# Attention stage: scores of the next sequence and probabilities of this one in one TensorE step

## The reference, cut to what matters

```python
x = x + layernorm(attn(layernorm(x), Wq, bq, Wk, bk, Wv, bv, Wo, bo))

def attn(x, ...):                       # B=16 sequences, S=256, hidden=256
    q = (x @ Wq.T + bq).reshape(B, S, 16, 16)   # 16 heads of 16
    k = (x @ Wk.T + bk).reshape(B, S, 4, 16)    # 4 key and value heads
    v = (x @ Wv.T + bv).reshape(B, S, 4, 16)
    q, k = rope(q), rope(k)
    scores = q @ k.T * 0.25, causal mask        # 4 query heads share a key head
    return (softmax(scores) @ v) @ Wo.T + bo
```

## Time and profile before

| | us |
|---|---|
| median of 3 runs | 2287.17 |
| lowest, highest run | 2286.58, 2296.49 |
| profiled execution | 2282.91 |
| its span, first to last instruction | 2281.2 |
| of that, from the first mask of the scores to the end of the attention stage (23.7 to 551.7) | 528.0 |

### The profile page before, as it was taken

The page is one execution under the profiler, slowest core; times in us unless marked ns, Lnnn a source line. Parts: engine busy times, 40 slices in busy tenths (PEclk is TensorE's granted clock), DMA queues, the critical chain, the costliest instruction groups (busy, mean ns, idle before and its releaser), DMA issues.

```text
span 2281.2 us, 35483 instructions
## 1 busy us (share of the span) xinstructions
PE 2082.8 (91%) x10450; PEld 1487.2 (65%) x10499; DVE 1319.4 (58%) x3916; ACT 740.1 (32%) x1495; POOL 271.7 (12%) x427
## 2 busy tenths in 40 slices
PE   7999999997599888884599999999999999999998
PEld 3544455444577555553377887778877788778887
DVE  3565665654533222222867777677777777677653
ACT  1233323332144322232333333333433343333321
POOL 1000000001055233332000000000000000000000
PEclk9899989988599999997689999999999999999999
DMA  9800000000022222224011101111011110111100
GB/s 341 160 1 0 0 0 0 0 0 1 2 93 92 74 76 78 76 76 175 14 52 56 52 17 45 56 56 51 5 56 56 51 56 5 56 56 38 42 21 31
DMA packets 75715, 120.74 MB, mean 53 GB/s; under 512 B 18672, under 2 KB 59760, under 8 KB 75120
## 3 DMA queue, kind: packets, MB, share of 16 engines
q1 hardware_dynamic: 68720, 100.91, 13.8%
q0 software_dynamic: 6912, 18.92, 2.3%
HBM read 81.71 MB, written 38.08 MB: 53 GB/s over the span
## 4 chain that ended last, share of the span: by engine, by line
PE 83%; issue 5%; DVE 5%; DMA 4%; ACT 2%; POOL 1%; SPq 0%; DVEq 0%; POOLq 0%; ACTq 0%
PE bank L184 21%; PE bank L193 11%; PE bank L1146 5%; PE bank L1175 5%; DMA moe_rows<-sorted_in 4%; PE bank L561 3%; PE bank L1185 3%; PE bank L1620 2%; PE bank L617 2%; PE bank L1646 2%; PE bank L1108 2%; PE bank L579 2%; PE bank L637 2%; PE bank L524 2%; PE bank L1599 2%
## 5 line engine op out<-in xcount | busy, mean ns | idle before, releaser
L184 PE MATMUL bank<-moe_xT,up_w 128*128 128x256 f32 x2304 | 554.1, 384 | 0.0
L184 PEld LDWEIGHTS bank<-moe_xT,up_w 128*128 128x128 f32 x2304 | 435.0, 191 | 70.3 <-issue 11.6
L193 PE MATMUL bank<-down_w,moe_hT 128*128 128x256 f32 x1152 | 307.6, 390 | 18.4 <-ACT moe_y L230 18.4
L227 ACT ACTIVATE moe_silu<-bank 128x256 f32<-128x256 f32 x288 | 110.6, 384 | 641.2 <-PE bank L184 641.2
L193 PEld LDWEIGHTS bank<-down_w,moe_hT 128*128 128x128 f32 x1152 | 202.9, 190 | 55.2 <-issue 26.5
L1325 DVE TENSOR_REDUCE q_slots<-bank 128x4 f32<-128x1024 f32 (+1 forms) x96 | 116.3, 1222 | 126.2 <-PE bank L1146 126.2
L1251 ACT ACTIVATE probs<-bank 128x1024 f32<-128x1024 f32 x96 | 98.4, 1025 | 201.1 <-PE bank L1175 201.1
L617 PE MATMUL bank<-up_w,moe_xT 128*128 x320 | 115.7, 485 | 25.3 <-issue 24.8
L1146 PE MATMUL bank<-kT,qT 16*128 16x256 f32 (+1 forms) x1024 | 125.4, 377 | 0.0
L293 DVE TENSOR_TENSOR moe_silu<-moe_silu,up_w 128x256 f32<-128x256 f32 x192 | 81.3, 423 | 75.2 <-ACT moe_silu L227 71.8
L1861 DVE TENSOR_TENSOR_SCAN m<-bank,delta 128x256 f32<-128x256 f32 x128 | 86.6, 677 | 64.7 <-PE bank L1660 63.4
(11 more groups left out here) (291 smaller groups left out, 3262.9 us busy)
## 6 DMA issues: line engine op xcount, KB each, us to landing
up_w<-comb_rows SPq DMA_DIRECT2D x32, 768.0 KB, 5.2
comb_got<-results SPq DMA_DIRECT2D x16, 768.0 KB, 7.9
moe_rows<-sorted_in SPq DMA_DIRECT2D x80, 128.5 KB
sorted_in<-zero SPq DMA_DIRECT2D x10, 1024.0 KB, 9.2
down_w<-comb_rows SPq DMA_DIRECT2D x16, 512.0 KB, 7.8
up_w<-in_up SPq DMA_DIRECT2D x2, 3168.0 KB, 14.1
up_w<-in_up SPq DMA_DIRECT2D x2, 2304.0 KB, 13.0
results<-moe_y SPq DMA_DIRECT2D x32, 128.0 KB
```

Of the source, the lines that this page charges most:

```text
L184: last = mm(k.bank[:, UP_BANK + i % 3, half * S:(half + 1) * S], m.w_up[:, c, at + half * m.inter:at + (half + 1) * m.inter], m.xT[:, par, ...
L193: last = mm(k.bank[:, SUM_BANK, j * D:(j + 1) * D], m.hT[:, i % 3, j * P:(j + 1) * P], m.w_down[:, m.expert(i), :], start=(i == 0 and j == ...
L227: nc.scalar.activation(m.silu[:, i % 3, :], k.bank[:, UP_BANK + i % 3, 0:S], ACT.Silu).then_inc(m.silu_ready, 1)
```

## The change

- A new step `pair` takes the place of `scores` and `probs` on TensorE. It issues, for i = 0 to 5, the scores of unit i of sequence t + 1 and the probabilities of unit i XOR 1 of sequence t, alternating. Since i and i XOR 1 are on different heads, the four products address the four row groups.
- PSUM is dealt out anew: banks 0 and 1 for scores, 2 and 3 for probabilities, 4 and 5 for `av`, 6 (`MIX_BANK`) for `turn_x`, `qkv`, `turn_att` and now `proj`, 7 for all turns of q and k. Scores have one pair of banks instead of two, and so have probabilities: pair i waits for the maxima and the exponentials of pair i - 1.
- `av` is three steps of four heads instead of six of two; `probs` has four buffers.
- `xn` and `z` (the two normalisations) move from VectorE to ScalarE, as an activation with a scale and a shift; GpSimd makes the shift with two small operations more. The residual (`add`) moves from VectorE to GpSimd. The copy of v (`copy_v`) moves from VectorE to ScalarE. The four additions of q in `rope` become one, the eight multiplications of `att` two.
- A sequence is now in work over five periods (norm at t - 3, statistics at t + 2); the table is walked from t = -1 to 17.

The core of the diff:

```diff
 ORDER = (
-    (0, "scores", 0), (0, "scores", 1), (0, "scores", 2), (0, "turn_m", 0), (-1, "att", 0), (-1, "turn_av", 1),
...
+    (0, "pair", 0), (1, "scores", 0), (0, "probs", 0), (-1, "turn_av", 1), (-1, "att", 0), (2, "qkv", 0), (1, "copy_v", 0),
+    (-2, "z", 0),
+    (0, "pair", 1), (1, "scores", 1), (0, "probs", 1), (2, "rope", 0), (-1, "turn_att", 0), (-2, "add", 0), (0, "av", 0),
+    (0, "pair", 2), (1, "scores", 2), (0, "probs", 2), (3, "norm", 0), (0, "copy_av", 0), (2, "qkv", 1), (1, "turn_m", 0),
+    (0, "pair", 3), (1, "scores", 3), (0, "probs", 3), (2, "rope", 1), (-1, "proj", 0), (2, "turn_q", 0), (-2, "stat", 0),
+    (0, "pair", 4), (1, "scores", 4), (0, "probs", 4), (3, "xn", 0), (0, "turn_av", 0), (2, "turn_q", 1), (-1, "post", 0),
+    (0, "av", 1),
+    (0, "pair", 5), (1, "scores", 5), (0, "probs", 5), (2, "turn_k", 0), (3, "turn_x", 0), (0, "av", 2), (0, "copy_av", 1),
+    (1, "turn_m", 1),
 )
...
+        if what == "pair":
+            scores, probs = within(t + 1), within(t)
...
+                pe.wait_ge(m.qT_ready, 2 * s + qb + 1)
+                pe.wait_ge(m.kT_ready, s + 1)
+                if begun(UNITS * s + i):
+                    pe.wait_ge(m.max_ready, UNITS * s + i)
...
+                pe.wait_ge(m.qmT_ready, 2 * t + pqb + 1)
+                if begun(UNITS * t + i):
+                    pe.wait_ge(m.probs_ready, UNITS * t + i)
...
+            for n in range(PAIR * REP):
+                r, lane = divmod(n, PAIR)
+                if scores and r < per:
+                    rows = slice(SLOT * heads[lane], SLOT * heads[lane] + HD)
+                    last = mm(k.bank[:, SCORE_BANK + lane, r * keys:(r + 1) * keys], m.qT[rows, its, qb, half * per + r, :],
+                              m.kT[rows, its, 0:keys], start=False, stop=(r == per - 1), skip_group_check=True)
...
+                if probs and r == 0:
+                    rows = slice(SLOT * pheads[lane], SLOT * pheads[lane] + HD + 1)
+                    last = mm(k.bank[:, PROB_BANK + lane, :], m.kT[rows, par, phalf * P:(phalf + 1) * P],
...
         if what == "av":
-            pe.wait_ge(m.probs_ready, UNITS * t + i + 1)
+            pe.wait_ge(m.probs_ready, UNITS * t + PAIR * i + PAIR)
...
         if what == "turn_att":
             pe.wait_ge(m.att_ready, t + 1)
...
+            if within(t + 3):
+                pe.wait_ge(m.qkv_read, 2 * t + 7)
...
         if what == "proj":
-
             pe.wait_ge(m.attT_ready, t + 1)
+            if within(t + 3):
+                pe.wait_ge(m.qkv_read, 2 * t + 8)
...
+        if what == "add":
+            pool.wait_ge(m.z_ready, t + 1)
+            x = cols(k.x, t, SEQ_TILES * D)
+            g.tensor_tensor(x, x, m.y[:].rearrange("p j d -> p (j d)"), ALU.add).then_inc(m.x_done, 1)
```

More of the change, by code:

```diff
@@ L1039, in unit @@
     return min(turn, 1), max(turn - 1, 0), range(pair * PAIR, (pair + 1) * PAIR)
+SCORE_BANK, PROB_BANK, AV_BANK, MIX_BANK, TURN_Q_BANK = 0, 2, 4, 6, 7
 ORDER = (
[L1045 to L1048 removed]
@@ L1051, with attention_period @@
+    (0, "pair", 3), (1, "scores", 3), (0, "probs", 3), (2, "rope", 1), (-1, "proj", 0), (2, "turn_q", 0), (-2, "stat", 0),
[3 more added lines that the diff above has]
+    (1, "turn_m", 1),
 )
-def attention_order(t, par, first, last):
+def attention_period(t, par):
     for ahead, what, i in ORDER:
-        if not (ahead == -1 and first or ahead == 1 and last):
+        here = (0, 1) if what == "pair" else (ahead,)
+        if not isinstance(t, int) or any(0 <= t + a < SEQS for a in here):
@@ L1057, in attention_order @@
             yield what, t + ahead, (par + ahead) % 2, i
 def attention_head(self):
[L1061 to L1065, removed]
+    for s in (0, 1):
+        for what, i in (("norm", 0), ("xn", 0), ("turn_x", 0)):
+            yield what, s, s, i
+        if s == 0:
+            for what, i in (("qkv", 0), ("rope", 0), ("qkv", 1), ("rope", 1), ("turn_q", 0), ("turn_q", 1), ("turn_k", 0)):
+                yield what, s, s, i
@@ L1068, in attention_pair @@
+    for t in (-1, 0, 1):
+        yield from attention_period(t, t % 2)
 def attention_pair(self, it):
-    yield from attention_order(2 * it + 2, 0, False, False)
-    yield from attention_order(2 * it + 3, 1, False, False)
+    for j in (0, 1):
+        yield from attention_period(2 * it + 2 + j, j)
 def attention_rest(self):
[L1074 to L1077, removed]
+    for t in range(SEQS - 4, SEQS + 2):
+        yield from attention_period(t, t % 2)
@@ L1262, in step @@
                 act.wait_ge(m.proj_full, t)
-            nc.scalar.copy(m.attT[:].rearrange("p c t -> p (c t)"), k.bank[:, 6, :]).then_inc(m.attT_ready, 1)
+            copy(m.attT[:].rearrange("p c t -> p (c t)"), mix).then_inc(m.attT_ready, 1)
+        if what == "z":
+            act.wait_ge(m.post_rstd, t + 1)
+            for j in range(SEQ_TILES):
+                last = activation(m.y[:, j, :], m.y[:, j, :], ACT.Identity, bias=m.pshift[:, j:j + 1],
+                                  scale=m.prstd[:, j:j + 1])
+            last.then_inc(m.z_ready, 1)
     go_through(m, act, step)
```

271 lines of the change are left out of this document (134 added, 137 removed).

## The result

| | before | after |
|---|---|---|
| median of 10 runs | 2282.75 us | 2295.77 us |
| lowest, highest run | 2275.18, 2296.49 | 2290.47, 2299.70 |
| span of the profiled execution | 2281.2 | 2294.6 |
| attention stage, first mask of the scores to the end of the last statistics | 23.7 to 552.1 | 27.4 to 535.8 |
| ScalarE's first `moe_y` copy of the last stage (L230) | 1236.6 | 1214.6 |

The changed kernel takes 1.0049 of the time before (95% interval 1.0031 to 1.0067; the two medians of the table alone give 1.0057): no gain, and if anything a loss, where 2224 us were forecast. The table shows two separate misses. The attention stage ends only 16 us earlier (its last instruction ends at 552.1 before, 0.4 us behind the 551.7 used above, and at 535.8 after) instead of 61.5.

What follows compares the result with a forecast made beforehand. TensorE was taken as the bound: its 22.3 us plus waits of 2.0, 2.0 and 0.4 made periods of 26.7 against 30.43. Attention summed to 473, 490 with clock falls, gaining 61.5: 2224 us, range 2212 to 2236.

Steps and rivals of the forecast that it cites:

- The bound, and the pair step: Attention: TensorE's steps bound the period; twelve product steps become six pair steps, 7.0 us less a period.
- Rivals 2 and 3: Pair products on four row groups: only partly at once (2246 us, chance 0.14), or taking turns altogether (2296, chance 0.04).
- rival 2: Pair step: four groups run only partly at once, some 0.25 us more a step: 2246 us, chance 0.14.
- TensorE's own work: Attention period without waits: 30.43 - 7.0 - 1.35 + 0.2 = 22.3 us.
- The waits: Attention: TensorE idle 2.0 us ahead of `turn_att`, 2.0 ahead of `proj`, 0.4 ahead of last `av`; period 26.7 us.
- The clock: Attention: falls to half clock in about half of the periods, 2.5 us each, 17 us with the ends.
- My own sign that I was wrong: Attention: TensorE idle under 1 us a period, or the lower clock covering more than a quarter of the stage.
- Rival 4: Attention: clock falls behind pair 1 and stays low for long, slower than before: 2326 us, chance 0.05.
- The ends of the stage: Attention: scores start at 26.0 us; first periods 27 and 22, t = 14 21.5, t = 15 18, last sequence 12.
- The later stages keep their length: Stages behind attention start earlier at unchanged length, apart from their own clock falls, some 5 us either way.
- The sum: Attention ends at 490 us instead of 551.7, gain 61.5: 2221.4 us as profiled, 2224 taken for the median.

Runs made afterwards that it cites:

- the early read: Changed kernel with VectorE's read of bank 6 as its own step ahead of the reduction of pairs 1 and 3: 2198.53 us, 0.9629 of before.
- the kernel with filler: Changed kernel with its two waits kept and 8 idle matmuls ahead of both `turn_att` and `proj`: 2253.45 us, 0.9871 of before.

## Why the prediction was wrong

Point by point, in its order.

- *The bound, and the pair step*: right. Two sets of products start on four row groups within 20 ns (309.11 to 309.13 above), and a pair's products take 1.07 to 1.10 us to the next step at full clock (211.17 to 212.24 above). Rivals 2 and 3 are out: four groups take no longer than two did. That two groups reach the full factor, as rival 2 says, no run shows. TensorE's own work was forecast at 22.3 us a period; with the early read it is busy for 22.45. The Trainium skill (TensorE: Matmul & The Clock Gate, Measured speedup vs the span model) has a measured 3.07 for four row groups; an estimate from it made a step 0.26 us longer. The trace does not agree for this mix of lengths: 1.07 to 1.10 us, against 1.06 to 1.07 on two groups.
- *The waits*: right in place and size, 1.90 and 1.86 us for 2.0 each, 0.3 to 0.4 ahead of the last `av`. With them but without falls a period is 26.6 us (forecast 26.7); without them 23.3.
- *The clock*: the step that failed. I took falls in half of the periods at 2.5 us, 17 us in the stage; they cost 48. The error is in how they were counted: I took each wait by itself and the stretch behind it as repaired by the next `qkv` or `proj`. Measured, nearly every wait brings a fall (23 of 25), the clock returns within 3.4 to 6.8 us, and the next wait takes it away again. The periods are 31.5 or 29.8 us, mostly in turn. The next `qkv` does not bring the clock back: it ran at half itself (2.93 us at 305.09). My own sign that I was wrong, more than a quarter of the stage at the lower clock, was just met: a mean granted clock of 0.87 over the stage, and 17.0 of 61.3 us in the two periods. Rival 4 had the mechanism (slower by the clock) but not this form; it needed two fifths of the time.
- *The ends of the stage*: 15 us too short. By the kernel with filler, the first products of the scores at 28.6 us (the sum starts at 26.0; 1.0 of the difference is their masks), the two first periods 28.6 and 23.7 us (27 and 22 forecast), t = 14 24.3 (21.5), and 36.2 from the start of t = 15 to the end (30).
- *The later stages keep their length, 5 us either way*: failed by 35 us, through a cause that stood in no part of the sum: that a change of VectorE's program in attention moves its later code was put at nothing. The stage between, the sparse one, was within it (5.7 us gained).
- *The sum*, for an execution like the profiled one: 2221.4 + 31 (clock) + 15 (ends) + 35 (the last stage) - 6 (the stage between) = 2296.4. The profiled execution took 2296.34, the median is 2295.77. The 2224 of the forecast is a slip of its own: 4.3 us for the median on top of 2221.4 make 2225.7, and the ten runs of before show no such distance (2282.75 against 2282.91).

Of the changes made in attention, then, the pair step and the wider `av` together were worth 7 us a period (30.4 to 23.3), and two properties of VectorE's program took it back: the read behind the reduction, and 29 instructions fewer ahead of the last loop.

## What to carry to other kernels

A short wait in a period that repeats is to be priced with the clock: here two gaps of 1.9 us cost 3.3 us as time and 4 us more as falls, and moving VectorE's read ahead of the reduction, in two places, gave back both. When a stage that nobody touched gets slower, look for idle time "issue" at one instruction of its loop, above all the first behind the jump back, and shift the engine's code by some idle instructions: it is a cheap test. And a change in one stage should be measured at two alignments of the later loops, or 30 us of luck, as here, are taken for its merit or its fault.

## What the runs showed of the hardware

- With two idle stretches of 1.9 us a period TensorE's clock fell behind 23 of 25 of them: 17.0 of 61.3 us at 1.2 GHz. With one a period it was 3.4 of 54.7 us; with none, no fall in 280 us, and none in 320 us where idle matmuls filled them.
- Products of 256 columns on one pair of row groups and of 512 on the other run together at no loss: 1.07 to 1.10 us for both, where either took 1.06 to 1.07 alone.
- Behind the jump back of a loop of some 580 VectorE instructions the next instruction comes 2.8 to 3.5 us later, in every kernel here; behind those of the loops of 9 to 28 instructions in the stages between it is 0.2 to 0.3 us.
- That loop can stall once a turn for 4 us at its first operation, up to 7.5 us under a burst of loads: it did with 959 and 1087 instructions ahead of it, and did not with 988 and 1010. Where in the fetch the time goes is not settled: the 8 KB instruction packets themselves take 0.3 to 0.5 us each, and what holds them, or the request for them, no view shows.
